# A four-layer transformer stack on one core: token rows loaded first on two queues, the sorted rows normed in two parts, and key and weight work placed around them

## The reference

```python
x = x + experts(layernorm(x), token_ids, ctx)       # 4 experts; the weights of expert e are ctx[e]
x = x + fp8_ffn(layernorm(x), w8)                   # x and w8 scaled by their largest value, rounded to e4m3
x = x + cross_attention(layernorm(x), ctx, Wq, bq, Wkv, bkv, Wp, bp)   # 16 heads, 1024 keys, q/k/v/attn fake-quantized
x = x + layernorm(x) @ ternary(w).T + bias          # w > t: 1, w < -t: -1, else 0; t = 0.7 mean|w| of a row

def expert(h, W):            # a token's expert is chosen by its token id
    g = silu(h @ W.T); u = h @ W.T; return (g * u) @ W.T

k, v = split(ctx @ Wkv + bkv)                       # 1024 rows x 512
k = clip(round(k / s), -127, 127) * s               # s = max|k| / 127 over a head's 16 values, v: over all keys
```

## Time and profile before

| | |
|---|---|
| median of 3 runs | 312.78 us (309.01 to 313.67) |
| the profiled execution | 313.84 us |
| its span, first to last instruction | 311.9 us |
| mean granted TensorE clock | 0.91 |
| DVE busy | 257.1 us (82%), 393 instructions |
| PE busy | 226.5 us (73%) |
| ACT busy | 204.3 us (65%) |
| POOL busy | 175.5 us (56%) |
| chain that ended last | POOL 23%, ACT 21%, DVE 19%, issue 19%, PE 10%, DMA 6% |

### The profile page before, as it was taken

The page is one execution under the profiler, slowest core; times in us unless marked ns, Lnnn a source line. Parts: engine busy times, 40 slices in busy tenths (PEclk is TensorE's granted clock), DMA queues, the critical chain, the costliest instruction groups (busy, mean ns, idle before and its releaser), DMA issues.

```text
span 311.9 us, 6380 instructions
## 1 busy us (share of the span) xinstructions
PE 226.5 (73%) x2212; PEld 158.3 (51%) x2242; DVE 257.1 (82%) x393; ACT 204.3 (65%) x352; POOL 175.5 (56%) x354
## 2 busy tenths in 40 slices
PE   4996558676767875797777778777876777775980
PEld 3544436464544761165555555555554555554760
DVE  2660989969779499999999999999997989999760
ACT  1100023544495636999999999999998899997120
POOL 2270244537642101477776867777676577777654
PEclk9999999979566797579999999999998999998696
DMA  7935000006999609989989989999989879989121
GB/s 249 301 107 154 1 1 0 2 0 128 189 185 183 128 0 188 199 120 185 162 158 147 154 163 167 151 144 185 155 152 139 115 160 152 165 157 162 23 70 67
DMA packets 133809, 41.07 MB, mean 132 GB/s; under 512 B 126353, under 2 KB 132881, under 8 KB 133777
## 3 DMA queue, kind: packets, MB, share of 16 engines
q1 hardware_dynamic: 131680, 37.24, 67.0%
q0 software_dynamic: 768, 2.10, 1.9%
q10 hardware_dynamic: 1328, 1.32, 1.3%
HBM read 5.25 MB, written 2.10 MB: 24 GB/s over the span
## 4 chain that ended last, share of the span: by engine, by line
POOL 23%; ACT 21%; DVE 19%; issue 19%; PE 10%; DMA 6%; POOLq 0%; ACTq 0%; DVEq 0%
POOL gates L473 10%; ACT ctxT L639 10%; ACT ctx L639 9%; POOL ebias L462 5%; DMA ksplit<-in_x 4%; POOL scratch L406 2%; POOL rstd L412 2%; PE ps L1160 2%; DVE nmax L969 2%; POOL out L499 2%; PE ps L1302 2%; DMA xs<-scratch 2%; PE ps L1392 2%; PE ps L1284 1%; DVE gates L847 1%
## 5 line engine op out<-in xcount | busy, mean ns | idle before, releaser
L969 DVE TENSOR_REDUCE nmax<-ps 128x1 f32<-128x1024 f32 x128 | 152.6, 1218 | 8.6 <-PE ps L1302 7.1
L1302 PE MATMUL ps<-keysT,kv 128*128 128x512 bf16 x226 | 75.8, 410 | 39.4 <-ACT ctx L639 25.0
L473 POOL CAST gates<-ksplit 128x512 int16<-128x512 uint8 x128 | 78.2, 612 | 11.5 <-DMA ksplit<-ctxT 3.1
L639 ACT ACTIVATE ctx<-ps,ebias,qscale 128x1024 uint8<-128x1024 f32 x64 | 76.8, 1202 | 6.2 <-POOL ebias L462 6.1
L639 ACT ACTIVATE ctxT<-ps,ebias,qscale 128x1024 uint8<-128x1024 f32 x64 | 76.5, 1200 | 1.8 <-POOL ebias L462 1.5
L462 POOL TENSOR_SCALAR ebias<-nmax,qscale 128x1 f32<-128x1 f32 x128 | 34.1, 267 | 41.8 <-DVE nmax L969 38.6
L1327 PEld LDWEIGHTS ps<-identb 128*128 128x128 bf16 x400 | 31.1, 99 | 25.0 <-issue 1.9
L1302 PEld LDWEIGHTS ps<-keysT,kv 128*128 128x128 bf16 x256 | 15.1, 99 | 50.4 <-ACT ctx L639 26.9
L1327 PE MATMUL ps<-identb 128*128 128x128 bf16 x400 | 39.4, 222 | 0.9 <-POOL gates L473 0.9
L532 ACT COPY hT<-ps 128x256 f32<-128x256 f32 x11 | 4.1, 372 | 45.7 <-PE ps L1152 45.7
L1334 PE MATMUL ps<-vals,gates 128*128 128x16 f16 x512 | 22.5, 170 | 0.0
(11 more groups left out here) (189 smaller groups left out, 356.9 us busy)
## 6 DMA issues: line engine op xcount, KB each, us to landing
keysT<-zeros SPq DMA_DIRECT2D x4, 512.0 KB, 8.1
ctx<-in_ctx SPq DMA_DIRECT2D x2, 512.0 KB, 5.0
ksplit<-in_x ACTq DMA_DIRECT2D x1, 1024.0 KB, 10.9
xs<-scratch SPq DMA_DIRECT2D x1, 1024.0 KB, 5.6
wkv_s<-in_L_xattn_Wkv SPq DMA_DIRECT2D x1, 512.0 KB, 8.3
ksplit<-ctx SPq DMA_TRANSPOSE x32, 3.8
ksplit<-ctxT SPq DMA_TRANSPOSE x32, 3.8
bkv_b<-in_L_xattn_bkv ACTq DMA_DIRECT2D x1, 256.0 KB, 11.4
```

The lines of the kernel that those rows point to most:

```text
L473: g.tensor_copy(byteT[:, w % PT, part, :, :], rawT[:, w % PAIRS, part, :].bitcast(U8).rearrange("p b (q j) -> p b j q", j=2)).then_inc(unp ...
L639: a.activation(probs, s_in, ACT.Exp, bias=ebias[:, u % 4:u % 4 + 1], scale=qscale[:, t, u:u + 1], accum_out=lsum[:, t, u:u + 1]).then_inc( ...
L969: v.tensor_reduce(nmax[:, u % 4:u % 4 + 1], score_banks(k, u), AX.X, ALU.max, negate=True).then_inc(max_ready, 1)
L1302: last = m.matmul(ps[:, bank + b, :], qT[:, t, u // 2, :], keysT[:, u % 2, u // 2, 512 * b:512 * b + 512], start=True, stop=True)
```

## The change

- The load of x is made in two halves: the first from SP ahead of the ctx and wkv loads, the second from ACT. SP then waits for both halves before it issues the loads of w8, wt, wq, wp and the biases.
- The sorted rows come back in two DMAs, tiles 0 to 2 (`EARLY` = 3) and 3 to 7, and DVE's sums, POOL's roots and DVE's norms are made in two parts. The first sums come after the add of kv row 5, the first norms after row 7. The sums and norms of tiles 3 to 7 move into step 0 of the expert loop, around kmax.
- The ternary weight moves from step 5 to behind the add of kv row 4 on DVE, and its turn on PE to the end of the kv loop. ACT, not DVE, copies `w8T` and `wtT`, before the first `copy_hT`.
- ACT takes over the scaling of `wp_s` in step 7 (from a new small tile `vunit`) and the copy of `vinv` in step 8. The places in PSUM get semaphores of their own.
- PE's keep_warm groups before the first job are 8 and 8, not 40, 24 and 20, its first job waits for `wtT_ready`, and it no longer waits for the sorted rows themselves.

```diff
@@ -35,6 +35,7 @@
+EARLY = 3
@@ -319,9 +323,11 @@
+            sp.dma_start(record[:, 0:NT // 2, 0:D], x_v[:, 0:NT // 2, :]).then_inc(ld_x, 16)
             for g in range(2):
...
             sp.dma_start(wkv_s[:, :, :], wkv.rearrange("(c p) n -> p c n", p=P)).then_inc(ld_wkv, 16)
+            sp.wait_ge(ld_x, 32)
             sp.dma_start(w8_s[:, :, :], w8.rearrange("(c p) n -> p c n", p=P)).then_inc(ld_w8, 16)
@@ -329,7 +335,8 @@
             sp.wait_ge(scattered, 16 * NT)
-            sp.dma_start(xs[:, :, :], sorted_v[:, :, 0:D]).then_inc(ld_sorted, 16)
+            sp.dma_start(xs[:, 0:EARLY, :], sorted_v[:, 0:EARLY, 0:D]).then_inc(ld_early, 16)
+            sp.dma_start(xs[:, EARLY:NT, :], sorted_v[:, EARLY:NT, 0:D]).then_inc(ld_sorted, 16)
             sp.dma_start(token_of[:, :].unsqueeze(2), sorted_v[:, :, D:D + 1].bitcast(I32),
@@ -401,7 +408,7 @@
-            pool.wait_ge(ld_x, 16)
+            pool.wait_ge(ld_x, 32)
@@ -416,7 +423,9 @@
             pool.wait_ge(sums1_ready, 1)
-            inverse_root(0, NT, rstd_ready)
+            inverse_root(0, EARLY, rstd_ready)
+            pool.wait_ge(sums1_ready, 2)
+            inverse_root(EARLY, NT, rstd_ready)
             pool.wait_ge(h_ready, NT)
@@ -441,7 +450,7 @@
-            pool.wait_ge(wide_used, 5)
+            pool.wait_ge(vinv_ready, 1)
@@ -517,7 +526,7 @@
-            act.dma_start(record[:, :, 0:D], x_v).then_inc(ld_x, 16)
+            act.dma_start(record[:, NT // 2:NT, 0:D], x_v[:, NT // 2:NT, :]).then_inc(ld_x, 16)
@@ -550,6 +559,22 @@
+
+            act.wait_ge(w8T_full, 1)
+            a.copy(w8T[:, :, :].rearrange("p c n -> p (c n)"), ps[:, 5, :].bitcast(BF16)[:, 0:C * D]).then_inc(w8T_ready, 1)
+            act.wait_ge(wtT_full, 1)
+            a.copy(wtT[:, :, :].rearrange("p c n -> p (c n)"), ps[:, TRB[0], :]).then_inc(wtT_ready, 1)
+
+            def value_scales(s):
+
+                if s == 7:
+                    act.wait_ge(ld_wp, 16)
+                    act.wait_ge(vunit_ready, 1)
+                    for c in range(C):
+                        a.activation(wp_s[:, c, :], wp_s[:, c, :], ACT.Copy, scale=vunit[:, c:c + 1]).then_inc(scaled_wp, 1)
+                if s == 8:
+                    act.wait_ge(vinv_full, 1)
+                    a.copy(vinv[:, :], ps[:, 7, 0:D]).then_inc(vinv_ready, 1)
@@ -563,6 +588,7 @@
                 key_parts(s)
+                value_scales(s)
                 for t in tiles_at(s - 1):
@@ -755,40 +781,52 @@
                     fp8_round(w8t, w8e, w8q[:, :, :].rearrange("p c n -> p (c n)"), w_ready)
-                if r == KT - 1:
-                    wide_wait()
-                    wide_free(v.tensor_copy(w8T[:, :, :].rearrange("p c n -> p (c n)"),
-                                            ps[:, 5, :].bitcast(BF16)[:, 0:C * D]))
-
-            def first_norm_sums():
-                dve.wait_ge(ld_sorted, 16)
-                for t in range(NT):
+                if r == 4:
+                    dve.wait_ge(ld_wt, 16)
+                    step(v.tensor_reduce(thr[:, :], wt_s[:, :, :], AX.X, ALU.add, apply_absolute_value=True))
+                    v.tensor_scalar(nthr[:, :], thr[:, :], 1.0 / D, -0.7, ALU.mult, ALU.mult)
+                    step(v.tensor_scalar(thr[:, :], thr[:, :], 1.0 / D, 0.7, ALU.mult, ALU.mult))
+                    for c in range(C):
+                        last = v.tensor_scalar(wlow[:, c, :], wt_s[:, c, :], nthr[:, c:c + 1], None, ALU.is_lt)
+                    step(last)
+                    for c in range(C):
+                        last = v.scalar_tensor_tensor(wtern[:, c, :], wt_s[:, c, :], thr[:, c:c + 1], wlow[:, c, :],
+                                                      ALU.is_gt, ALU.subtract)
+                    last.then_inc(w_ready, 1)
+
+            def first_sums(lo, hi):
+                dve.wait_ge(ld_early if hi <= EARLY else ld_sorted, 16)
+                for t in range(lo, hi):
                     v.bn_stats(stats[:, t, :], xs[:, t, :]).then_inc(dve_done, 1)
-                n[0] += NT
+                n[0] += hi - lo
                 dve.wait_ge(dve_done, n[0])
-                for t in range(NT):
+                for t in range(lo, hi):
                     last = v.bn_aggr(mv[:, t, :], stats[:, t, :])
...
+            def first_norm(lo, hi, roots):
+                dve.wait_ge(rstd_ready, roots)
+                for t in range(lo, hi):
+                    v.tensor_scalar(hs[:, t, :], xs[:, t, :], mv[:, t, 0:1], rstd[:, t:t + 1],
+                                    ALU.subtract, ALU.mult).then_inc(h_ready, 1)
...
                 v.tensor_tensor(kv[:, r, :], ps[:, KVB[r % 4], :], bkv_b[:, :], ALU.add).then_inc(kv_ready, 1)
-                if r == NORM_AT:
-                    first_norm_sums()
                 weights(r)
-            dve.wait_ge(kv_ready, KT)
+                if r == 5:
+                    first_sums(0, EARLY)
+            first_norm(0, EARLY, 1)
             kk = kv[:, :, 0:D].rearrange("p r (h d) -> p r h d", d=HD)
-            dve.wait_ge(rstd_ready, 1)
-            for t in range(NT):
-                v.tensor_scalar(hs[:, t, :], xs[:, t, :], mv[:, t, 0:1], rstd[:, t:t + 1],
-                                ALU.subtract, ALU.mult).then_inc(h_ready, 1)
...
                 if s == 0:
+                    first_sums(EARLY, NT)
+                    dve.wait_ge(kv_ready, KT)
                     step(v.tensor_reduce(kmax[:, :, :], kk, AX.X, ALU.max, apply_absolute_value=True))
+                    first_norm(EARLY, NT, 2)
                     step(v.tensor_scalar(kscale[:, :, :], kmax[:, :, :], 1.0 / 127.0, 1e-8, ALU.mult, ALU.max))
@@ -806,34 +844,11 @@
                     step(v.tensor_scalar(vscT[:, :], vmaxT[:, :], 1.0 / 127.0, 1e-8, ALU.mult, ALU.max))
+                    v.tensor_scalar(vunit[:, :], vscT[:, :], HALF_UNIT, None, ALU.mult).then_inc(vunit_ready, 1)
                     step(v.reciprocal(vinvT[:, :], vscT[:, :]))
...
                     last.then_inc(vdiag_ready, 1)
-                if s == 5:
-                    dve.wait_ge(ld_wt, 16)
-                    step(v.tensor_reduce(thr[:, :], wt_s[:, :, :], AX.X, ALU.add, apply_absolute_value=True))
-                    v.tensor_scalar(nthr[:, :], thr[:, :], 1.0 / D, -0.7, ALU.mult, ALU.mult)
-                    step(v.tensor_scalar(thr[:, :], thr[:, :], 1.0 / D, 0.7, ALU.mult, ALU.mult))
-                    for c in range(C):
-                        last = v.tensor_scalar(wlow[:, c, :], wt_s[:, c, :], nthr[:, c:c + 1], None, ALU.is_lt)
-                    step(last)
-                    for c in range(C):
-                        last = v.scalar_tensor_tensor(wtern[:, c, :], wt_s[:, c, :], thr[:, c:c + 1], wlow[:, c, :],
-                                                      ALU.is_gt, ALU.subtract)
-                    last.then_inc(w_ready, 1)
-                if s == 9:
-                    wide_wait()
-                    wide_free(v.tensor_copy(vinv[:, :], ps[:, 7, 0:D]))
-                if s == 8:
-
-                    dve.wait_ge(ld_wp, 16)
-                    for c in range(C):
-                        last = v.tensor_scalar(wp_s[:, c, :], wp_s[:, c, :], vscT[:, c:c + 1], HALF_UNIT, ALU.mult, ALU.mult)
-                    last.then_inc(scaled_wp, 1)
-                if s == JOBS + 1:
-                    wide_wait()
-                    wide_free(v.tensor_copy(wtT[:, :, :].rearrange("p c n -> p (c n)"), ps[:, 7, :]))
@@ -1123,7 +1138,13 @@
-                    last.then_inc(wide_full, 1)
+                    last.then_inc(w8T_full, 1)
+                    pe.wait_ge(w_ready, 4)
+                    for c in range(C):
+                        for i in range(C):
+                            last = m.transpose(ps[:, TRB[0], i * D + c * P:i * D + (c + 1) * P],
+                                               wtern[:, c, i * P:(i + 1) * P], identf[:, :])
+                    last.then_inc(wtT_full, 1)
@@ -1169,26 +1190,17 @@
-                    pe.wait_ge(wide_used, 4)
+                    pe.wait_ge(wide_used, 3)
...
-                    last.then_inc(wide_full, 1)
-                if s == JOBS + 1:
-                    pe.wait_ge(w_ready, 4)
-                    pe.wait_ge(wide_used, 5)
-                    for c in range(C):
-                        for i in range(C):
-                            last = m.transpose(ps[:, 7, i * D + c * P:i * D + (c + 1) * P],
-                                               wtern[:, c, i * P:(i + 1) * P], identf[:, :])
-                    last.then_inc(wide_full, 1)
...
+                    last.then_inc(vinv_full, 1)
...
-                    pe.wait_ge(wide_used, 3)
+                    pe.wait_ge(w8T_ready, 1)
@@ -1196,11 +1208,10 @@
-            keep_warm(40, 1)
-            pe.wait_ge(ld_sorted, 16)
-            keep_warm(24, 1)
+            keep_warm(8, 1)
...
-            keep_warm(20, 1)
+            keep_warm(8, 1)
+            pe.wait_ge(wtT_ready, 1)
@@ -1222,10 +1233,10 @@
```

(11 more changed lines are left out.)

## The result

The changed kernel takes 313.94 us (median of 20 runs, 311.78 to 316.17) where the kernel before takes 311.67 (20 runs, 309.01 to 314.42). The ratio is 1.0085, 95% interval 1.0063 to 1.0107: slower by a little under one per cent. The forecast was 307.7, range 303.8 to 311.0. It is wrong in direction, and the time lies outside the range.

The account below looks back on a forecast made before the run. Bound: a serial chain of waits to the first tile, then DVE, later POOL. Shifts of 2.0 and 3.1 sum to 5.1 off the profiled 313.84: 308.7, or 307.7 beside the median; range 303.8 to 311.0.

Parts of the forecast that it names:

- the signs of being wrong: Whole profile: DMA wait of DVE on xs, kv products from 13 or later, ACT ahead of second norms, late-stage length changed.
- Part 2: DVE and PE up to the first tile: hT(0) at 31.0 against 37.20, 6.2 us earlier.
- the ctx term: Loads on SP's queue: half of x ahead of ctx delays the kv products by 0.7 us, bounds 0 to 1.6.
- Part 1: Loads: split x starts the scatters at 8.2 to 9.0, not 13.10; first rows land by 26.9; kv products from 11.7.
- registers 2.34: PE before hT(0): reading the eight tile_expert registers was charged 2.34 us, the idle time in the earlier trace.
- PE's own route: PE before hT(0): products end at 26.3, turns until 27.6, then register reads and two warm groups, giving 31.0.
- Rival (c): Step 0: PE idles from about 37.3 to 42.7, then half clock costs up to 2 us; 310.6 in all; 18%.
- Part 3: Step 0: added sums and norms put the second gate at 42.3, 3.1 earlier; a step 1 stall leaves 2.0.
- my full stall: Step 1: the kq TENSOR_SCALAR waits for POOL's memset until 45.9, which makes the shift 1.5 us.
- Part 4: Loop from step 5: without the ternary work, POOL's first single-column root comes 3.1 us earlier, bounds 2.3 to 4.2.
- (b): Whole kernel: no step 1 stall, ctx not delayed, last expert product at 2.4 GHz; 7.9 us gained, 304.9; 25%.
- (d): Head: scatters beside weight loads take twice 12.33, rows land near 37, DVE waits; 317.5, milder form 311 to 313; 7%.

Follow-up runs that it names:

- after, again: The changed kernel itself, unedited, measured and profiled a second time: 312.94 us.
- both repairs: Changed kernel with the eight register reads moved into the kv loop and 36 keep_warm transposes ahead of PE's wait for ctx: 307.12 us, ratio 0.986 to the kernel before.
- the early sums: Changed kernel with reads in the kv loop, 36 keep_warm transposes before ctx, and sums of tiles 3 to 7 ahead of the first gate: 306.21 us, ratio 0.983.
- reads moved: Changed kernel with PE's eight register reads of tile_expert moved into the kv loop, two behind each of rows 3 to 6: 310.07 us, ratio 0.987.
- old loads: Changed kernel with x loaded whole from ACT's queue and no SP wait, as before the change: 310.79 us, ratio 0.996.
- before again: The kernel before the change, unedited, measured and profiled a second time: 311.62 us.

## Why the prediction was wrong

The forecast's own milestones, in us from the span's start, beside the profiled executions:

| | forecast | after | after, again | both repairs |
|---|---|---|---|---|
| first scatter | 8.2 to 9.0 | 9.14 | 9.08 | 9.00 |
| kv products | 11.7 | 14.46 | 14.08 | 13.43 |
| first keep_warm before hT(0) | 29.9 | 36.61 | 34.21 | 28.62 |
| hT(0) | 31.0 | 38.29 | 35.88 | 31.92 |
| first gate | 34.1 | 42.70 | 40.30 | 34.95 |
| second gate | 42.3 | 50.77 | 48.36 | 43.02 |
| first single-column root | 67.2 | 75.19 | 72.91 | 67.41 |
| time of the profiled execution | 308.7 | 315.24 | 312.94 | 307.00 |

The loss at the first gate adds up. In the second profile of the changed kernel it is 6.2 behind the forecast: 2.4 for ctx (products at 14.08, not 11.7), 2.4 for the reads (4.77, not 2.34), 0.6 for the 16 warming transposes and 1.35 for the stretch from hT(0) to the gate, both at half clock, less 0.5 because the ternary matrix was turned sooner behind the products. In the first profile the slow kv products add 2.0, and ctx 0.4.

In the last column hT(0) and all later steps stand within 1.0 of the forecast. For hT(0) itself that is partly luck: the products start 1.7 late, the reads of 2.34 are hidden altogether, and PE then waits 1.2 for DVE's norm. What the column does show is that behind hT(0) the lengths of the forecast hold. The time is 1.7 under the forecast though the root is 0.2 behind it: the late stretch again, through which the forecast carried its shift unchanged, and whose change of length it had listed among the signs of being wrong. All that made the change a loss lies ahead of the first gate, in Part 2, in the ctx term of Part 1 and in the 3.07 from hT(0) to the gate.

**The step that failed first: "registers 2.34".** I took the idle time of the earlier trace rows for the duration of the reads. It was the part that stuck out from beneath the kv products; the reads take about 5.3. The change puts a wait of PE for the ternary weight ahead of them, so they can't begin until 31.2. This costs 2.4 more than was charged. It was shown from both sides, by moving the reads (gone) and by taking away the wait (2.28 again). PE's own route was rightly named as the one that decides; it was priced from the wrong row.

**The ctx term was too small.** 0.7 was charged, bounds 0 to 1.6; the turn of ctx starts 3.4 later and the products 3.1 to 3.5. The step was the estimate that 512 KB more on SP's queue cost 1.9, from two issues 0.5 apart and their landings. The undo of the loads alone shows the whole of it (ctx turned from 6.50, products at 10.90). Why the slope failed stays open: it is not just the bytes ahead of ctx on its own queue, since with ctx first there its second load still landed 9.4 us after its issue, where 5.7 was the longest before.

**Cover was counted once and not for what varies.** The forecast gave PE's products their 14.6 us as in the one profile. The 7.63 us wait of DVE had hidden a variation of 2.4 us in them; in the changed kernel it is on the path whenever it falls. Nor did the forecast allow for half rate from hT(0) to the first gate: 4.41 and not 3.07, at half clock (the column behind POOL's is the granted clock, 0.50 is 1.2 GHz; window of the changed kernel, columns as in the earlier trace rows):

```profile
36.00:42.00 6.00, 4.81 (x24) 3.54 (x24) 0.00 (x0) 0.37 (x1) 0.00 (x0) 0.50 0.01 3
```

PE stood idle for 4.78 right before it, but that alone does not settle it: with both repairs the stretch is 3.03 (31.92 to 34.95), and with the early sums it is 4.39 at half clock again, after 1.23 of idle time in both. Rival (c) named a clock fall, but placed it in step 1. There it came too (with both repairs PE idled for 5.74 and its granted clock was 0.50 from 44 to 48), but DVE waited only 0.33 for it, not up to 2.

**Part 3 was right in size.** From first to second gate I had 8.2; it is 8.06 or 8.07 in the changed kernel, in it again and with both repairs. kscale takes 0.22 (put at 0.2). The stall in step 1 is where the rule cited there and my own price differed. POOL's extra_mask copies took 1.18 and 0.64, where the same copies took 0.19 and 0.19 before; the first stood beside DVE's kq product, which has two SBUF inputs, the second beside the TENSOR_SCALAR of 52.92; the memset came at 53.79, as the TENSOR_SCALAR of 52.92 ended, which took 0.90 and not 0.69 and was not held for 1.8. So my full stall did not occur. The rule of the Trainium skill (SBUF — State Buffer, Who interferes with whom), that whichever comes first keeps the shared port, put that order right, and its shift would have been 2.6 at a first gate of 34.1. With both repairs the gate was 0.85 later than that and the shift at the third gate 2.0 (48.02 to 45.98). My 2.0 thus came out by two small errors of opposite sign.

**Part 4 was right.** 3.1 forecast, 2.9 measured (24.31 to 21.45), 2.9 again with both repairs (21.43), and undoing the ternary move alone takes it away (25.0).

**Rivals.** (b) and (d) did not occur: DVE never waited for the rows, which were issued at 21.85 and 22.27 and took 3.1 and 4.8. The case that did occur, PE's own chain becoming the bound at a worse price than charged, had no slower ending in my list. I had written that even with rows at once hT(0) could not come before 28.3, and did not ask what that number would be if its terms were wrong.

## What to carry to other kernels

An idle time in front of an instruction is what is left of a cost after its cover, not the cost. Before a wait is put ahead of sequencer work such as register reads, read that work's own rows for its whole duration, and see how far the sequencer had run ahead. When a long wait is removed, the chain that was hidden behind it takes over with everything that the wait absorbed: price that chain at its worst seen, and look for its spread in a second profile.

Here the repair was small: reading the registers between the products turns 0.9% slower into 1.3% faster. Keeping PE busy while ctx loads as well gives 1.4%, and the runs do not show that it adds anything.

## What the hardware showed that I had not expected

- A register read from SBUF on PE's queue takes 0.30 us, up to 0.49, and with its register operations 0.65 to 0.7; the transposes behind the eight reads began only after the last of them (28.33 before, 36.61 after).
- Whether the first eight kv products run in 3.67 or in 5.4 to 6.2 us is not set by the idle time before them. It was 3.67 with 4 us of idle time ahead of the ctx turn (reads moved, after again) and 6.1 with none (old loads, before again). After 36 keep_warm transposes it was 3.67 in three of three kernels. The profile's granted clock reads 1.00 from 14 to 18 us in the changed kernel, where only four of its products fall in 4 us, so there the pace tells more than the clock's row. What decides it is not settled. The row (columns as above):

```profile
14.00:18.00 4.00, 3.54 (x4) 1.51 (x5) 0.00 (x0) 0.36 (x1) 3.03 (x4) 1.00 0.94 221
```

- With half of x ahead of them on SP's queue the two loads of ctx landed 8.5 to 9.7 us after their issue. With half of x behind them the first took 3.8 and the second 9.4, and when ACT carried all of x they took 4.2 to 5.7. Why the second is so late with ctx first and less on ACT's queue stays open.
- One POOL copy of one column took 1.18 us beside a DVE product of two SBUF inputs, six times its usual 0.19.
